# Four PSUM banks for projections, the softmax exponential read from PSUM, and output biases as a matmul row

## What is computed

```
# attention 1: 16 heads of 64, softmax over the 77 keys of the own batch
q = x @ w_q;  k = cond @ w_k;  v = cond @ w_v
out = softmax(q k^T * 64**-0.5) v;   return out @ w_out + b_out
# attention 2: 8 heads of 128, batches merged: 616 keys for every query,
#   sim = (sim - mean) * 1.5 + mean ahead of the softmax
# attention 3: as attention 1, with 8 heads of 64
x = x + tanh(g_xattn[l]) * attention_l(layernorm(x), ctx, ...)
```

## Time and profile before

| | |
|---|---|
| Runs | 3338.55, 3341.37, 3346.36 us; median 3341.37 |
| Profiled execution | 3337.73 us; its span 3335.9 us |
| Mean granted clock of TensorE | 0.818 |
| Busy in the span | PE 68%, PEld 51%, DVE 61%, ACT 35%, POOL 31% |
| Attention 1 | from 1283 to 1633 us |
| Attention 2 | from 1997 to 2405 us |
| Attention 3 | from 2784 to 2960 us |

### The profile page before, as it was taken

The page is one execution under the profiler, slowest core; times in us unless marked ns, Lnnn a source line. Parts: engine busy times, 40 slices in busy tenths (PEclk is TensorE's granted clock), DMA queues, the critical chain, the costliest instruction groups (busy, mean ns, idle before and its releaser), DMA issues.

```text
span 3335.9 us, 56980 instructions
## 1 busy us (share of the span) xinstructions
PE 2270.2 (68%) x18576; PEld 1692.3 (51%) x18576; DVE 2029.3 (61%) x4720; ACT 1173.9 (35%) x2478; POOL 1040.5 (31%) x909
## 2 busy tenths in 40 slices
PE   0113334749159994676579967888669994759998
PEld 0111112615148783455468854666558883545555
DVE  8766664172764347776644446888665556664776
ACT  0211110004036562333256545666434333322322
POOL 5020000009616642444136622555326530011110
PEclk9955555579569996778689979999879996779999
DMA  3020003906448781655568843999857772210000
GB/s 98 8 45 0 0 0 108 295 0 214 164 154 265 221 223 51 167 151 151 139 204 257 228 142 81 223 226 226 188 174 234 230 197 54 50 45 19 19 0 25
DMA packets 404666, 440.04 MB, mean 132 GB/s; under 512 B 287090, under 2 KB 361330, under 8 KB 379890
## 3 DMA queue, kind: packets, MB, share of 16 engines
q1 hardware_dynamic: 333284, 361.08, 36.5%
q0 software_dynamic: 26496, 36.19, 6.4%
q10 hardware_dynamic: 44784, 41.55, 4.3%
HBM read 285.73 MB, written 85.92 MB: 111 GB/s over the span
## 4 chain that ended last, share of the span: by engine, by line
PE 42%; DVE 25%; issue 8%; DMA 7%; DVEq 7%; ACT 6%; POOL 1%; ACTq 1%; PEld 1%; SPq 1%; POOLq 1%; PEldq 0%
PE ps L974 11%; PE ps L991 8%; PE ps L188 7%; PE ps L189 6%; PE ps L190 6%; DMA arena<-arena 2%; DMA residual_rows<-arena 2%; DVE arena L1450 2%; DVEq L1482 2%; ACT arena L1414 2%; PE ps L290 1%; DVE bn_stats L231 1%; DVE arena L1943 1%; DMA arena<-s_kernel 1%; DVE arena L1627 1%
## 5 line engine op out<-in xcount | busy, mean ns | idle before, releaser
L2324 POOL TENSOR_SCALAR w_raw<-w_raw 128x1024 f32<-128x1024 f32 (+5 forms) x169 | 169.5, 1062 | 1468.1 <-DVEq L179 730.0
L974 PE MATMUL ps<-arena 128*128 128x256 f16 (+1 forms) x3864 | 511.8, 275 | 4.4 <-issue 4.4
L1042 DVE TENSOR_TENSOR arena<-ps,arena 128x256 f16<-128x256 f32 x506 | 214.4, 424 | 359.6 <-ACT arena L1020 332.9
L188 PE MATMUL ps<-arena 128*128 128x308 f16 (+5 forms) x1248 | 315.3, 280 | 164.9 <-ACTq L1424 28.4
L991 PE MATMUL ps<-arena 128*128 128x256 f16 x3036 | 423.5, 274 | 0.0
L974 PEld LDWEIGHTS ps<-arena 128*128 128x128 f16 (+1 forms) x3864 | 376.7, 100 | 62.1 <-issue 15.0
L991 PEld LDWEIGHTS ps<-arena 128*128 128x128 f16 x3036 | 290.2, 98 | 48.7 <-DVE arena L1042 9.2
L189 PE MATMUL ps<-arena 128*128 128x308 f16 (+5 forms) x1248 | 314.7, 279 | 0.0
L190 PE MATMUL ps<-arena 128*128 128x308 f16 (+5 forms) x1248 | 313.1, 277 | 0.0
L188 PE MATMUL ps<-xT,w_split 128*128 (+2 forms) x720 | 256.3, 356 | 70.4 <-DVE arena L1450 53.2
L1450 DVE SCALAR_TENSOR_TENSOR arena<-ps,arena 128x512 f16<-128x512 f32 (+3 forms) x258 | 159.6, 635 | 184.8 <-ACT arena L1414 183.8
(11 more groups left out here) (288 smaller groups left out, 4798.0 us busy)
## 6 DMA issues: line engine op xcount, KB each, us to landing
arena<-split_experts SPq DMA_DIRECT2D x46, 1088.0 KB
arena<-split_experts SPq DMA_DIRECT2D x46, 1028.0 KB
w_raw<-in_we SPq DMA_DIRECT2D x32, 1024.0 KB
arena<-s_kernel ACTq DMA_DIRECT2D x64, 512.0 KB, 4.9
split_experts<-w_staged SPq DMA_DIRECT2D x32, 1024.0 KB, 4.8
arena<-split_experts SPq DMA_DIRECT2D x23, 1408.0 KB
arena<-split_experts SPq DMA_DIRECT2D x23, 768.0 KB
w_raw<-in_we SPq DMA_DIRECT2D x16, 704.0 KB
```

Of the source, the lines that this page charges most:

```text
L188: pe.matmul(out_ap, lhs(0), rhs(0), start=start, stop=False)
L974: last = pe.matmul(F.up_out(k, j, g), F.wu(k, a_, g, d, j), F.xe[:, k, b_, d * TROWS:(d + 1) * TROWS], start=g == 0 and d == 0 and n == 0, ...
L1042: dve.tensor_tensor(F.hh[0:m, r, 1, :], hf, F.hh[0:m, r, 0, :], ALU.subtract).then_inc(F.s_h, 1)
L2324: pool.tensor_scalar(v, v, WSCALE, 1.0, ALU.mult, ALU.mult)
```

## The change

- Projections use four banks, 4 to 7, in turn; four are free at first. In attention 1 the second `out` of a batch counts three uses, so that a body has a multiple of four.
- In attentions 1 and 3 DVE makes the minimum only (q now carries the factor minus scale), and ACT takes the exponential from PSUM in four instructions of 77 elements, one for each head, with that minimum as bias. A bank of scores is free again when the exponentials have read it.
- There ACT takes the events of a step in another order where the step has no `out`: the copies of pv, v, q and k first, then the copy of the probabilities, then the exponentials. The high copy and the low half of the probabilities are one instruction for both tiles.
- The output biases move to a matmul of the bias rows with ones ahead of each `out`. DVE's additions at the starts and the broadcasting DMA go. POOL scales and splits three more rows at the kernel's start.

```diff
-                self.s_pfree = credit(n + "_proj_free", 2)
+                self.s_pfree = credit(n + "_proj_free", 4)
-                self.car, self.cex = (0, 2) if merged else (4, 0)
-                self.s_ar = sem(n + "_exp_arg") if merged else credit(n + "_exp_arg", 4)
-                self.s_ex = credit(n + "_exp_done", 2) if merged else sem(n + "_exp_done")
+                self.cex = 2 if merged else 4
+                self.s_ar = sem(n + "_exp_arg")
+                self.s_ex = credit(n + "_exp_done", self.cex)
...
+            def uses_first(self, T):
+
+                ev = self.events(T)
+                if self.merged or any(e[0] == "out" for e in ev):
+                    return ev
+                return [e for e in ev if e[0] in ("pv", "v", "q", "k")] + [e for e in ev if e[0] not in ("pv", "v", "q", "k")]
...
+            def count(self, key):
+
+                return 1 + self.pad if key[0] == "out" and key[2] == 1 else 1
-            def bank67(self, key):
-                return 6 + self.use[key] % 2
+            def bank(self, key):
+                return 4 + self.use[key] % 4
...
-                                      -3.0 * self.scale * INV if self.merged else INV)]))
+                                      (-3.0 if self.merged else -1.0) * self.scale * INV)]))
...
+                    pe.matmul(ps[:, A.bank(key), 0:D], ones[0:33, :], b2m[:, A.layer, :], start=True, stop=False)
...
-                    pe.wait_ge(A.s_ex if A.merged else A.s_ar, 2 * T + t + 1)
+                    pe.wait_ge(A.s_ex, 2 * T + t + 1)
...
-                            v = A.pr[:, r, t, :, :]
-                            act.activation(v, v, ACT.Exp, scale=A.scale).then_inc(A.s_ex, 1)
+                            for h in range(4):
+                                m = act.activation(A.pr[:, r, t, h, :], ps[:, 2 * r + t, h * G:(h + 1) * G], ACT.Exp,
+                                                   scale=-1.0, bias=A.mx[:, r, t, h:h + 1])
+                            m.then_inc(A.s_ex, 1)
...
+                        act.activation(A.heads(r, 0), A.pr[:, r, :, :, :], ACT.Copy).then_inc(A.s_hi, 2)
...
+                        dve.wait_ge(A.s_hi, 2 * T + 2)
+                        dve.tensor_tensor(A.heads(r, 1), A.pr[:, r, :, :, :], A.heads(r, 0), ALU.subtract).then_inc(A.s_lo, 2)
...
-                        dve.tensor_reduce(A.mx[:, r, t, :], src, X, ALU.max)
-                        dve.drain()
-                        dve.tensor_tensor(A.pr[:, r, t, :, :], src,
-                                          A.mx[:, r, t, :].unsqueeze(2).to_broadcast([P, 4, G]), ALU.subtract)\
-                            .then_inc(A.s_ar, 1)
+                        dve.tensor_reduce(A.mx[:, r, t, :], src, X, ALU.min).then_inc(A.s_ar, 1)
...
-                dve.tensor_scalar(brow[:, A.layer - 1, :], brow[:, A.layer - 1, :], tg[:, A.layer:A.layer + 1], None, ALU.mult)
...
-                with dve.Fori(0, NT) as t:
-                    dve.tensor_tensor(x[:, t, :], x[:, t, :], brow[:, A.layer - 1, :], ALU.add)
-                dve.drain()
...
-            sp.dma_start(brow[:].rearrange("p a b -> p (a b)"), a["brow"].partition_broadcast(P)).then_inc(s_const, 16)
+                sp.dma_start(b2r[r:r + 1, 17 * D:20 * D], a["brow"].rearrange("(a n) -> a n", a=1)).then_inc(s_tmp, 16)
```

More of the change, by code:

```diff
@@ L1205, in plan @@
                 self.use, self.high = {}, {}
+                n_use = 0
+                self.pad = -sum(k in ("k", "v", "q", "out") or (k == "pv" and not self.merged) or k == "pvhalf"
+                                for k, b, g in bodies[self.h]) % 4
                 for k, b, g in self.first + [e for x_ in bodies for e in x_] + self.tail:
@@ L1208, in plan @@
                         key = (k, b, g) if k != "pvhalf" else ("pv", b, g + 1)
-                        self.use[key] = len(self.use)
+                        self.use[key] = n_use
+                        n_use += self.count(key)
                         if k != "out":
@@ L1213, in plan @@
                 self.sh = self.high["pv", 3, 1] - self.high["pv", 2, 1]
-                assert self.su % 2 == 0
+                assert self.su % 4 == 0
             def walk(self, fori, eng):
+                on_act = isinstance(eng, AttnACT)
+                bodies, tail = (self.bodies_act, self.tail_act) if on_act else (self.bodies, self.tail)
                 for e in self.first:
                     eng.event(*e, 0)
-                for body in self.bodies[:self.h]:
+                for body in bodies[:self.h]:
                     for e in body:
@@ L1223, in walk @@
                 with fori(0, B - 1 - self.h) as i:
-                    for e in self.bodies[self.h]:
+                    for e in bodies[self.h]:
                         eng.event(*e, i)
-                for e in self.bodies[B - 1] + self.tail:
+                for e in bodies[B - 1] + tail:
                     eng.event(*e, 0)
@@ L1244, in entry, with heads @@
                 return kv[e] if k in ("kv", "k") else kv[self.NC // 4 + e]
-            def heads(self, v):
-                return v.rearrange("p (h k) -> p h k", h=4)[:, :, 0:G]
+            def heads(self, r, half):
+                return self.hl[:, r, :, half, :].rearrange("p t (h k) -> p t h k", h=4)[:, :, :, 0:G]
             def wq(self, h, k, c):
@@ L1413, in event @@
                     for view, dst, scale in A.entry(k, b, g, i)[1] if k != "pv" else [A.odrain(g)]:
-                        m = act.activation(dst(0), view(A.bank67(key)), ACT.Copy, scale=scale)
+                        m = act.activation(dst(0), view(A.bank(key)), ACT.Copy, scale=scale)
                     m.then_inc(A.s_ph, 1)
@@ L1431, in event @@
                     act.wait_ge(A.s_p, T + 1)
-                    for t in range(2):
-                        if A.merged:
-                            m = act.activation(A.hl[:, r, t, 0, 0:GA], A.pr[:, r, t, :], ACT.Copy, scale=A.sm[:, r, t, 1:2])
-                        else:
-                            m = act.activation(A.heads(A.hl[:, r, t, 0, :]), A.pr[:, r, t, :, :], ACT.Copy)
-                        m.then_inc(A.s_hi, 1)
+                    if A.merged:
+                        for t in range(2):
+                            act.activation(A.hl[:, r, t, 0, 0:GA], A.pr[:, r, t, :], ACT.Copy, scale=A.sm[:, r, t, 1:2])\
+                                .then_inc(A.s_hi, 1)
+                    else:
+                        act.activation(A.heads(r, 0), A.pr[:, r, :, :, :], ACT.Copy).then_inc(A.s_hi, 2)
         class AttnDVE:
@@ L1449, in event @@
                     for view, dst, scale in A.entry(k, b, g, i)[1] if k != "pv" else [A.odrain(g)]:
-                        m = dve.scalar_tensor_tensor(dst(1), view(A.bank67(key)), scale, dst(0), ALU.mult, ALU.subtract)
+                        m = dve.scalar_tensor_tensor(dst(1), view(A.bank(key)), scale, dst(0), ALU.mult, ALU.subtract)
                     m.then_inc(A.s_pfree, 1)
@@ L1468, in event @@
                     xo = x[:, 2 * (b + i) + g, :]
-                    dve.scalar_tensor_tensor(xo, ps[:, A.bank67((k, b, g)), 0:D], sm[:, 4, 0:1], xo, ALU.mult, ALU.add)\
-                        .then_inc(A.s_pfree, 1)
+                    dve.scalar_tensor_tensor(xo, ps[:, A.bank((k, b, g)), 0:D], sm[:, 4, 0:1], xo, ALU.mult, ALU.add)\
+                        .then_inc(A.s_pfree, A.count((k, b, g)))
             def maxima(self, T, g, r):
```

57 lines of the change are left out of this document (28 added, 29 removed).

## The result

| | before | changed |
|---|---|---|
| Median | 3342.61 us (4 runs) | 3231.18 us (4 runs, 3220.62 to 3239.20) |
| Ratio | | 0.9665, 95% interval 0.9635 to 0.9695 |
| Profiled execution | 3337.73 us, span 3335.9 | 3239.2 us, span 3237.4 |
| Mean granted clock | 0.818 | 0.84 |

The account below looks back on a forecast made before the run. Bound by a ring of copies, subtractions and two banks in attentions 1 and 3, DMA in attention 2. Gains of 80 (attention 1), 39 (attention 3), 17 (attention 2) and 2.5 (start) total 138: 3337.7 to 3200 us, range 3155 to 3262.

Parts of the forecast that it names:

- What bounds it: Attentions 1 and 3: no engine full, a ring of ScalarE copies, VectorE subtractions and two TensorE banks; attention 2: DMA.
- Bias rows at the starts: Starts of attentions 1, 2, 3: dropping VectorE's bias additions gives back about 15, 13 and 5 us.
- The broadcast at the kernel's start: Kernel start: removing the bias broadcast load that ScalarE waited for saves 2.5 us, bounded by 0 and 4.
- Denser POOL work: Attention bodies: POOL's denser work beside VectorE costs an estimated 0.1 us a step, not in the sum.
- Exponential from PSUM: Attentions 1 and 3: VectorE saves 0.94 us a step; ScalarE's small exponentials take 0.24 us each.
- Four banks and the order, attention 1: Attention 1's bodies: VectorE's copy waits vanish; 40.5 us becomes 28.6 at full clock, 31.4 at clock 0.85.
- Attention 3: Its bodies, reckoned like attention 1's: 19.9 us becomes 13.7 at full clock, 15.3 at 0.85; 39 us for the stage.
- The clock: TensorE in attentions 1 and 3: shorter idle gaps raise the mean granted clock from 0.77 and 0.72 to 0.85.
- A: Rival: VectorE alone bounds, TensorE stays at full clock; bodies 28.6 and 13.7 us, 164 us gained, 3174; chance 0.18.
- B: Rival: the clock sinks to 0.65; bodies 36.1 and 18.0 us, 93 us gained, 3245; chance 0.20.
- C: Rival: only the starts gain; exponentials of 0.46 us or more and a low clock leave bodies unchanged; about 3298; chance 0.09.
- D: Rival: slower, as transposes enter ScalarE's ring; about 3350 us at a landing of 14 us; chance 0.03.

Follow-up runs that it names:

- e3: The changed kernel with the old ScalarE order in all attentions and only two of the four banks free at a time; 3314.52 us, ratio 0.9921.
- e8: The changed kernel with the old ScalarE order in attention 3 and the exponential as before (VectorE subtracts, ScalarE reads SBUF); 3233.04 us, ratio 0.9685.
- e1: The changed kernel with the old order of ScalarE's events in attention 3 only; 3207.81 us, ratio 0.9622.
- e4: The changed kernel, its ScalarE order kept, with the k projection ahead of the outs in attention 3; 3208.88 us, ratio 0.9631.
- e5: The changed kernel with, in attention 3, both k ahead of the outs and the old ScalarE order; 3211.05 us, ratio 0.9622.
- e2: The changed kernel with the old ScalarE order in all three attentions, four banks kept; 3224.27 us, ratio 0.9675.

## Why the prediction was right and wrong, step by step

- *What bounds it.* Right. The ring of copies, subtractions and two banks was the bound: with two banks kept (e3) attention 1 falls 7 us, with four 60, with the new order 74 to 80.
- *Bias rows at the starts.* Right. From memset to the first maximum, attention 2 fell from 53.2 to 39.7 us with two banks (e3), 13.5 against a forecast of 13, and to 35.2 with four, 4.5 against 4. The bodies of attention 2, which I gave nothing, moved by no more than they repeat: from first maximum to last out 354.4 us before, 352.2 after, 350.8 to 355.1 in other runs with four banks. With two (e3) they take 358.1, so the bias matmuls may cost something there that the banks give back; one profile does not show it.
- *The broadcast at the kernel's start.* Wrong in sign. The load was what the start waited for, and VectorE did start 1.7 us earlier; but "the longer bias work of POOL lies under the generation of the first stage's kernel" failed: it lies beside it and holds VectorE up. +4.8 where -2.5 stood. The section of the Trainium skill that I cited for POOL's splitting ("SBUF — State Buffer", Who interferes with whom) says of VectorE's 2-port modes that whoever issues first has the shared ports for the whole instruction and the other blocks; of an instruction with two SBUF inputs it says that it contends. 9.99 beside 9.85 us agrees with blocking for the whole instruction. I applied it only to the bodies.
- *Denser POOL work.* My estimate of 0.1 us a step was too small, in the direction that I gave. In attention 1 POOL is busy 0.44 of the time before and 0.56 after. VectorE's normalise, with both inputs in SBUF, lasts 0.80 us in attention 3, where POOL is idle; in attention 1 it went from 914 ns to 1298:

```profile
L1498 DVE TENSOR_TENSOR arena<-arena 128x616 f32<-128x616 f32 x24 | 21.9, 914 | 1.8
```

```profile
L1514 DVE TENSOR_TENSOR arena<-arena 128x616 f32<-128x616 f32 x20 | 26.0, 1298 | 1.5
```

  The low half of the probabilities, in the same way, is 0.43 us a step over its time in attention 3 before and 0.29 after. Together POOL cost VectorE 0.55 us a step before and 0.79 now, an estimate from these means: 0.24 more. The subtractions, with one input in PSUM, lasted 479 ns in both attentions.
- *Exponential from PSUM.* Right: 0.23 us each against 0.24, and taking the subtractions back costs 14 to 21 us in attention 1 (e8), of the 30 that 0.94 us a step would give. It pays only with the banks: with two of them the body was 41.3 us without subtractions (e3).
- *Four banks and the order, attention 1.* Right in size: a body of 31.4 us, forecast 31.4. That the two are equal is in part luck. The clock was 0.92 where I took 0.85, and by my own formula that would have given 30.0; the waits were longer. Steps without outs take mostly 5.9 to 6.7 us (up to 8.8), but those with outs 10.2 to 12.6, 11.4 in the mean, where 9.4 at full clock was forecast. In the step at 1410 the outs start after an idle stretch of TensorE of 3.38 us. The first matmuls still stand 0.11 us apart; from 1410.64 to 1413.6 they stand 0.21 apart, the low clock, which costs some 1.5 us of that step.

```profile
1409.44 0.28 PE L1381 MATMUL ps<-b_mlp_out,ones 33*128 33x256 f16 x1 [3.38 <-DVE arena L1471]
```

- *Attention 3.* The step that failed is "For attention 3 alike: 19.9 - 5.9 - 1.9 = 12.1 of VectorE, plus some 1.6 of waits". Two things are not alike. With two steps a batch, k is made in the last step before its use, so scores wait for its low half, and pv, v and q of the step come behind. And the new order then puts the copy of the probabilities behind q. The body, forecast 15.3, was 20.5 in the middle of the stage and 19.9 by the count that my 19.9 of before came from; either edit brings the 20.5 to 16.9 or 17.4 (e1, e4). Over VectorE's own 12.1 us the forecast had 3.2, of waits and clock together; e1 has waits for projection copies of 4.3, at a clock of 0.79 where I gave 0.85. With 0.89 (e5) they are no shorter.
- *The clock.* Right in direction in attention 1, and too low: 0.92 against 0.85. With the old order it was 0.79 with two banks and 0.86 with four (e3 and e2, five bodies each):

```profile
1375.00:1581.30 206.30, 146.49 (x1270) 106.62 (x1270) 120.79 (x200) 84.82 (x250) 93.55 (x60) 0.79 0.55 153
```

```profile
1353.00:1525.20 172.20, 133.02 (x1271) 101.71 (x1270) 126.79 (x200) 82.83 (x250) 88.53 (x62) 0.86 0.66 183
```

  In attention 3 it stayed at 0.74, and once the late fill was gone it was 0.79 to 0.90, with the same four banks. The rule on cycling through banks ("TensorE: Matmul & The Clock Gate" of the Trainium skill, A second HAM failure mode), read as in the prediction, would have kept the share at full clock from rising in both. So the trace does not bear it out for this change.
- *The rivals.* A and B did not come: attention 1's body is between theirs. Attention 3's, 19.9 us, is past even B's 18.0, at a clock of 0.74 where B has 0.65, so it is not B's mechanism. C is excluded by attention 1's body, 9 us shorter, and by the exponential's 0.23 us. D's mechanism, transposes in ScalarE's ring, is there in the trace of the changed kernel as a wait of TensorE for the transposes of 3.8 us at most (total us, times, longest, from 1330 to 1560 us). It does not decide: with the old order (e2) TensorE has no such wait from 1345 to 1530 us, against 6.2 us with the new one, and attention 1 is longer.

```profile
PE ps L187 <- DMA arena<-arena: 16.5, 9, 3.8
```

## What to carry to other kernels

When an engine's events are put in a new order, follow each shape of the loop by itself: the order that gave about 16 us with four steps a batch took 21 with two, where a value is made in the last step before its use. Moving uses ahead of a copy pays only if what fills them is never late; ask for the latest input of the things moved ahead. And price work that goes to POOL as work beside VectorE, above all long rows on one partition, which cost as much as on 33.

## What the runs showed of the hardware

- A POOL instruction of 5120 elements takes 4.6 us on one partition and 4.6 us on 33, and a VectorE instruction of 256 elements that meets one ends with it (9.99 beside 9.85 us, 9.81 over two beside another).
- A VectorE instruction with both inputs in SBUF lasts longer where POOL works beside it (128x616 f32: 0.80 us with POOL idle, 0.91 with POOL busy 0.44 of the time, 1.30 with 0.56); one with an input in PSUM does not (128x308: 0.48 in both).
- Eight exponentials of 77 elements from PSUM in a row take 1.82 us, 0.23 each, though each row says 0.34.
